# Cross-attention scores from stacked high and low parts, and a router that reads unsplit tokens, in a two-layer decoder on one core

## What is computed

```python
# E: cross-attention, 16 heads of 16 columns
q = (x @ Wq + bq);  k = (ctx @ Wk + bk);  v = (ctx @ Wv + bv)      # each split into 16 heads
attn = softmax(clip(q @ k.T * 16 ** -0.5, -1e4, 1e4))
x = layernorm(x + (attn @ v) @ Wo + bo)
# F: router and experts
gate = softmax(x @ gate_w)                       # 8 experts, top 2 of each token
...
```

## Time and profile before

| | us |
|---|---|
| median of 3 runs (1593.13 to 1594.19) | 1593.33 |
| the profiled execution, its own time | 1595.76 |
| its span (what the trace covers) | 1594.0 |
| stage E, first to last score reduction | 928.4 to 1194.7 |
| closing of the last two batches, up to the last scatter | to 1247 |
| stage F (experts) | from about 1260 |

### The profile page before, as it was taken

The page is one execution under the profiler, slowest core; times in us unless marked ns, Lnnn a source line. Parts: engine busy times, 40 slices in busy tenths (PEclk is TensorE's granted clock), DMA queues, the critical chain, the costliest instruction groups (busy, mean ns, idle before and its releaser), DMA issues.

```text
span 1594.0 us, 23807 instructions
## 1 busy us (share of the span) xinstructions
PE 1365.7 (86%) x9303; PEld 1151.7 (72%) x9303; DVE 1114.1 (70%) x1885; ACT 560.8 (35%) x1122; POOL 804.4 (50%) x751
## 2 busy tenths in 40 slices
PE   5787799989989989989989789988894299999990
PEld 5786678868877877877666567766664299999990
DVE  5888776686676667654545568877783488888886
ACT  2354311021121121113333334444342266666652
POOL 3333456556556655642101123544555478888852
PEclk8897799999999999999999979989886599999995
DMA  5100133223322322310000000000000466566624
GB/s 167 31 11 16 47 93 102 95 84 101 98 69 90 96 80 86 97 58 28 1 1 1 6 6 1 13 13 23 8 8 14 147 240 212 216 236 227 208 70 158
DMA packets 44974, 129.83 MB, mean 81 GB/s; under 512 B 8406, under 2 KB 23225, under 8 KB 38976
## 3 DMA queue, kind: packets, MB, share of 16 engines
q1 hardware_dynamic: 32688, 66.70, 13.3%
q0 software_dynamic: 12176, 61.63, 10.9%
HBM read 119.82 MB, written 10.31 MB: 82 GB/s over the span
## 4 chain that ended last, share of the span: by engine, by line
PE 60%; DVE 22%; issue 6%; ACT 5%; POOL 3%; DMA 2%; SPq 0%; ACTq 0%; DVEq 0%; POOLq 0%
PE bank L399 13%; PE bank L401 12%; PE bank L400 12%; PE bank L1204 8%; PE bank L407 4%; PE bank L1039 3%; PE bank L1098 2%; PE bank L1025 2%; DVE topE L1731 2%; DVE hid_hi L1604 2%; DVE shiftE L1738 2%; DVE hf L1623 1%; PE bank L1120 1%; ACT feat L1356 1%; PE bank L1052 1%
## 5 line engine op out<-in xcount | busy, mean ns | idle before, releaser
L1606 DVE TENSOR_TENSOR hid_lo<-hf,hid_hi 128x512 fp32r<-128x512 f32 x96 | 219.8, 2290 | 3.3
L526 POOL TENSOR_TENSOR wpiece_lo<-wraw,wpiece_hi 128x1024 fp32r<-128x1024 f32 x88 | 215.9, 2453 | 7.4
L399 PE MATMUL bank<-hid_hi,wpiece_lo 128*128 128x512 f32 x512 | 200.5, 392 | 10.8 <-DVE hid_lo L1606 10.8
L400 PE MATMUL bank<-hid_lo,wpiece_hi 128*128 128x512 f32 x512 | 199.3, 389 | 0.0
L401 PE MATMUL bank<-hid_hi,wpiece_hi 128*128 128x512 f32 x512 | 199.3, 389 | 0.0
L524 POOL TENSOR_SCALAR wpiece_hi<-wraw 128x1024 fp32r<-128x1024 f32 x88 | 94.1, 1070 | 195.0 <-PE bank L401 191.0
L1604 DVE CAST hid_hi<-hf 128x512 fp32r<-128x512 f32 x96 | 77.6, 808 | 123.2 <-ACT hf L1306 122.1
L1306 ACT ACTIVATE hf<-bank,ffn_scales 128x512 f32<-128x512 f32 x64 | 44.2, 690 | 291.2 <-PE bank L401 291.2
L433 POOL TENSOR_TENSOR lnM_rstd<-lnM_rstd,minus_half 128x2 f32<-128x2 f32 x24 | 16.9, 709 | 214.8 <-DVE lnM_rstd L427 195.6
L635 POOL TENSOR_SCALAR probE<-probE 128x1024 f32<-128x1024 f32 x64 | 66.6, 1042 | 112.7 <-ACT probE L1388 112.5
L399 PEld LDWEIGHTS bank<-hid_hi,wpiece_lo 128*128 128x128 f32 x512 | 96.1, 188 | 35.6 <-DVE hid_lo L1606 15.9
(11 more groups left out here) (327 smaller groups left out, 3887.8 us busy)
## 6 DMA issues: line engine op xcount, KB each, us to landing
wraw<-in_C_w SPq DMA_DIRECT2D x88, 512.0 KB, 3.6
yc<-y_rows SPq DMA_DIRECT2D x16, 256.0 KB, 5.4
ctx_raw<-in_ctxT SPq DMA_DIRECT2D x16, 192.0 KB, 2.9
xraw<-in_xT SPq DMA_DIRECT2D x8, 256.0 KB, 3.8
x_tok<-in_x SPq DMA_DIRECT2D x8, 256.0 KB, 4.2
x_rows<-x_tok SPq DMA_DIRECT2D x8, 256.0 KB, 2.1
out_x<-x_tok SPq DMA_DIRECT2D x8, 256.0 KB, 2.1
staging<-in_A_wqkv SPq DMA_DIRECT2D x1, 768.0 KB, 6.7
```

The lines of the kernel that those rows point to most:

```text
L399: pe.e.matmul(o, sl, mh, start=start and i == 0, stop=False)
L400: pe.e.matmul(o, sh, ml, start=False, stop=False)
L526: pool.e.tensor_tensor(pair[1], raw, f(pair[0]), ALU.subtract).then_inc(done, 1)
L1606: dve.e.tensor_tensor(lo[:, o, :], hf[o % 2][:, :], f(hi[:, o, :]), ALU.subtract).then_inc(s_hid, 1)
```

## The change

1. Scores. q and k are no longer evicted into the tiles that the scores read. ScalarE evicts each of them twice with the bias added: into `qk_hi` (rounded to fp32r) and into `qk_raw` (fp32). GpSimd subtracts to get `qk_lo`. SyncE writes both parts to internal memory in HBM (`split_qk`) and reads them back, rearranged: each head gets 64 partitions, four blocks of its 16 rows: high, high, low, low for q and high, low, high, low for k. One fp32r matmul over the 64 rows then sums all four products of parts. For each of q and k of a batch there are 2 writes (256 KB each) and 8 loads, each of 16 partitions by 8 KB (128 KB), in pieces of 1 KB; 160 DMAs in all. There is one `qk_raw`, `qk_hi`, `qk_lo`, so k's eviction waits for q's subtraction and q's writes.
2. k is no longer stored twice with zeros; heads come in plain order.
3. Router. In stage E ScalarE copies the transposed tokens straight from PSUM into `xtf`; the high and the low part are not made there, and GpSimd's sum is gone.
4. FIN's later steps move one round ahead. `prob_e` has four buffers instead of six. `mask_a` lies in another part of SBUF, and the small load of `of_parity` is gone.

Below, after the tiles, come the programs of GpSimd, SyncE, TensorE and ScalarE, in this order.

```diff
-        items.append((base + PAIRS + 8, 1, "FIN", (b,), (0, 2, 4, 6, 7, 9, 11, 11, 13)))
+        items.append((base + PAIRS + 8, 1, "FIN", (b,), (0, 2, 4, 6, 6, 8, 10, 10, 12)))
...
+        split_qk = ring(2, lambda i: nc.dram_tensor(f"split_qk{i}", (2, 2, D, S), F32, kind="Internal").ap())
...
-        q_e = ring(2, lambda i: sbe(f"qE{i}", [P, KC, S]))
-        k_e = ring(2, lambda i: sbe(f"kE{i}", [P, 2, KC, S]))
+        qk_raw, qk_hi, qk_lo = sbe("qk_raw", [P, KC, S]), sbe("qk_hi", [P, KC, S], F32R), sbe("qk_lo", [P, KC, S], F32R)
+        q_e = ring(2, lambda i: sbe(f"qE{i}", [P, PAIRS, S], F32R))
+        k_e = ring(2, lambda i: sbe(f"kE{i}", [P, PAIRS, S], F32R))
...
+                elif name == "PRE" and step < 3:
+                    b, = args
+                    n, u = 2 * b + step - 1, use["E", "qk"[step - 1], b]
+                    pool.wait_ge(u.drained, u.done)
+                    pool.wait_ge(w_qk, 32 * n)
+                    pool.e.tensor_tensor(qk_lo[:, :, :], qk_raw[:, :, :], f(qk_hi[:, :, :]), ALU.subtract).then_inc(s_qklo, 1)
...
-                    if step == 4:
-                        wait_xt(pool, "E", b)
...
-                        pool.e.tensor_tensor(xtf[:, :, :], f(xt_hi[:, :, cols]), f(xt_lo[:, :, cols]), ALU.add).then_inc(s_xtf, 1)
...
+            def stack_heads(b, which):
+
+                n, held = 2 * b + which, split_qk[b % 2][which]
+                if b >= 2:
+                    sp.wait_ge(l_qk[b % 2], 16 * 16 * (b // 2))
+                for part, (src, done) in enumerate(((qk_hi, s_qkhi), (qk_lo, s_qklo))):
+                    sp.wait_ge(done, n + 1)
+                    load(held[part].rearrange("(c p) s -> p c s", p=P), f(src[:, :, :]), w_qk)
+                sp.wait_ge(w_qk, 32 * (n + 1))
+                if b >= 2:
+                    old = use["E", "s", b - 2, PAIRS - 1]
+                    sp.wait_ge(old.filled, old.full)
+                for r in range(4):
+                    heads = held[(r % 2) if which else r // 2].rearrange("(j i d) s -> i d j s", i=2, d=DH)
+                    for i in range(2):
+                        load(f((k_e if which else q_e)[b % 2][(4 * i + r) * DH:(4 * i + r + 1) * DH, :, :]), heads[i], l_qk[b % 2])
...
-                    for key in "qk":
-                        pe.wait_ge(use["E", key, b].drained, use["E", key, b].done)
+                    pe.wait_ge(l_qk[b % 2], 16 * 16 * (b // 2 + 1))
                     pe.wait_ge(u.drained, u.turn)
                     for t in range(TT):
                         for i in range(2):
-                            c, par, g = e_head(p, i)
-                            rows = slice(32 * g, 32 * g + 32)
+                            rows = slice(i * 4 * DH, (i + 1) * 4 * DH)
                             o = u.ap[:, (i * TT + t) * S:(i * TT + t + 1) * S]
-                            made = pe.e.matmul(o, q_e[b % 2][rows, c, t * P:(t + 1) * P], k_e[b % 2][rows, par, c, :],
+                            made = pe.e.matmul(o, q_e[b % 2][rows, p, t * P:(t + 1) * P], k_e[b % 2][rows, p, :],
                                                start=True, stop=True)
...
+                    act.wait_ge(s_qklo, n)
+                    act.wait_ge(w_qk, 32 * n)
                     for c in range(KC):
-                        if step == 1:
...
+                        made = act.e.activation(qk_hi[:, c, :], u.ap[:, c * S:(c + 1) * S], ACT.Identity, bias=bias[:, c:c + 1])
+                    made.then_inc(s_qkhi, 1)
+                    for c in range(KC):
+                        made = act.e.activation(qk_raw[:, c, :], u.ap[:, c * S:(c + 1) * S], ACT.Identity, bias=bias[:, c:c + 1])
                     made.then_inc(u.drained, 1)
```

More of the change, by code:

```diff
@@ L248, in build @@
         resid = ring(3, lambda i: sb(f"resid{i}", [P, TT, D], F32, mid))
-        mask_a = sb("mask_a", [P, 3 * P], F32, mid)
         ctx_raw = ring(2, lambda i: sb(f"ctx_raw{i}", [CK, 2, S], F32, mid))
@@ L271, in build @@
         wqkv = hilo("wqkv", [P, KC, 3 * D], early)
+        mask_a = sb("mask_a", [P, 3 * P], F32, early)
         bqkv = sb("bqkv", [P, 6], F32, early)
@@ L330, in build @@
         ev, eo = hilo("ev", [CK, 2, D], part, "right"), hilo("eo", [P, KC, D], part, "right")
-        ebq, ebk, of_parity = sbp("ebq", [P, KC]), sbp("ebk", [P, 2 * KC]), sbp("of_parity", [P, 2])
+        ebq, ebk = sbp("ebq", [P, KC]), sbp("ebk", [P, KC])
         ebv, ebo = sbp("ebv", [P, D]), sbp("ebo", [P, D])
@@ L362, in build @@
         s_vone, s_prob = sem("e_ones"), sem("e_prob")
-        s_xtf, s_rm, s_re, s_rf, s_rb, s_rs, s_sh = (sem(f"r_{n}") for n in ("xtf", "m", "e", "f", "b", "s", "sh"))
+        s_qkhi, s_qklo, w_qk, l_qk = sem("e_qkhi"), sem("e_qklo"), sem("w_qk"), ring(2, lambda i: sem(f"l_qk{i}"))
+        s_rm, s_re, s_rf, s_rb, s_rs, s_sh = (sem(f"r_{n}") for n in ("m", "e", "f", "b", "s", "sh"))
         s_seen, s_slot = sem("r_seen"), sem("r_slot")
@@ L633, in pool_program @@
                     pool.wait_ge(u.drained, u.done)
-                    pr = prob_e[n % 6][:, :, :, :].rearrange("p i k s -> p (i k s)")
+                    pr = prob_e[n % 4][:, :, :, :].rearrange("p i k s -> p (i k s)")
                     pool.e.tensor_scalar(pr, pr, 1.0, 0.0, ALU.min, ALU.max).then_inc(s_prob, 1)
@@ L639, in pool_program @@
                     b, = args
-                    finish("E", step, b, ebo, l_eb, 80)
-                    if step == 4:
-                        wait_xt(pool, "E", b)
-                        if b:
-                            old = use["E", "l", b - 1]
-                            pool.wait_ge(old.filled, old.full)
-                        cols = slice(b * S, (b + 1) * S)
-                        pool.e.tensor_tensor(xtf[:, :, :], f(xt_hi[:, :, cols]), f(xt_lo[:, :, cols]), ALU.add).then_inc(s_xtf, 1)
-                    elif step == 6 and b < B - 1:
+                    finish("E", step, b, ebo, l_eb, 64)
+                    if step == 6 and b < B - 1:
                         one_hot(pool, b)
@@ L789, in sync_program @@
             load(ebo[:, :], a["E_bo"], l_eb)
-            load(of_parity[:, :], a["of_parity"], l_eb)
             sp.wait_ge(s_ew, 1)
@@ L802, in sync_program @@
                     load(ctx_raw[b % 2][:, :, :], a["ctxT"][:, :, b * S:(b + 1) * S], l_ctx[b % 2])
+                elif name == "PRE" and step < 3:
+                    stack_heads(b, step - 1)
                 elif name == "FIN" and step == 4:
@@ L1134, in tensor_program @@
                         pe.wait_ge(l_rt, 16 * 5)
-                        pe.wait_ge(s_xtf, b + 1)
+                        ux = use["E", "x", b]
+                        pe.wait_ge(ux.drained, ux.done)
                         pe.wait_ge(u.drained, u.turn)
@@ L1326, in finish @@
                     ln_apply(act, "M", B + n, b, resid[(B + n) % 3])
+                elif step == 3 and stage == "D":
+                    ln_hi(act, "M", B + n, b, use["D", "x", b])
                 elif step == 3:
-                    ln_hi(act, "M", B + n, b, use[stage, "x", b])
+                    u = use["E", "x", b]
+                    act.wait_ge(u.filled, u.full)
+                    if b:
+                        old = use["E", "l", b - 1]
+                        act.wait_ge(old.filled, old.full)
+                    act.e.activation(xtf[:, :, :], u.ap[:, :].rearrange("p (c t) -> p c t", c=KC), ACT.Identity).then_inc(u.drained, 1)
             for name, step, args in DS:
@@ L1693, in finish @@
                     ln_scale(dve, "M", k)
-                elif step == 3:
-                    ln_lo(dve, "M", k, b, use[stage, "x", b])
+                elif step == 3 and stage == "D":
+                    ln_lo(dve, "M", k, b, use["D", "x", b])
             for name, step, args in DS:
@@ L1723, in vector_program @@
                 if name == "PRE" and step == 3:
-                    dve.wait_ge(l_eb, 80)
+                    dve.wait_ge(l_eb, 64)
                     values("E", *args, ebv)
@@ L1951 @@
         proj[r:r + DH, h // 2, h % 2, :] = g[L1 + "attn_proj"][h]
-    of_parity = (np.arange(P)[:, None] // DH % 2 == np.arange(2)).astype(np.float32)
     laid = {
@@ L1957 @@
         "mask_d": np.concatenate([tri.T, np.ones((P, P), np.float32), tri.T], 1),
-        "of_parity": of_parity,
         "iota8": np.broadcast_to(np.arange(NE, dtype=np.float32), (P, NE)),
@@ L1980 @@
         "E_bq": cols(g[L1 + "xattn_bq"]),
-        "E_bk": np.where(of_parity[:, :, None] > 0, cols(g[L1 + "xattn_bk"])[:, None, :], 0).reshape(P, 2 * KC),
+        "E_bk": cols(g[L1 + "xattn_bk"]),
         "E_wv": rows(g[L1 + "xattn_Wv"], CK),
```

33 lines of the change are left out of this document (9 added, 24 removed).

## The result

| | before | after |
|---|---|---|
| median of the runs | 1593.76 us | 1704.76 us (1688.96 to 1712.03) |
| the profiled execution, its own time | 1595.76 | 1688.96 |
| its span | 1594.0 | 1687.2 |
| first and last score reduction | 928.4, 1194.7 | 942.3, 1297.8 |
| end of the last scatter | 1247.2 | 1337.6 |

The ratio of the changed kernel to the one before is 1.0685 (95% interval 1.0589 to 1.078): slower by 111 us at the median, by 93 in the profiled executions. One of the four executions of the kernel before took 1969.6 us and is left out of the ratio; the other three lay between 1593.13 and 1594.19. Measured again beside the experiments, at another time, it was 1.0589 (1.0519 to 1.0658).

A forecast was written before the change was run, and what follows sets the result against it. Neither engine was full: VectorE alternated between work and waits for scores. Start +26, batches 0 to 2 +40, 3 to 6 +24.6, batch 7 -1.5, router and closing -10: +79 on 1595.8, so 1674.9, median 1672; range 1585 to 1706 us.

The forecast's parts named there:

- batches 3 to 6: Stage E, later batches: period 43.5 us each, set by the way through memory, +24.6 us over 149.4.
- batches 0 to 2: Stage E, first batches: period 42.5 us each with the way through memory, +40 us over 87.5.
- L: Time of one set of eight loads of q or k: 12 us taken, between bounds 6.9 and 21.6.
- a wait put down to GpSimd's scatters instead of DMA: Sign of a wrong forecast: the wait for k in stage E comes from GpSimd's scatters, not DMA; no size given.
- time 0: Stage E: the scores of the round in which q is made; pair 0 is due five rounds later.
- The three rounds before time 0: Stage E, between a batch's pair 0 and the next time 0: about 9 us in batches 0 to 2, 10 later.
- Part 1: Scores on TensorE: cheaper by 0.56 us per pair; gain 2.4 us per batch in batches 3 to 6, 1.5 in batch 7.
- Part 3: Router and closing: router waits for GpSimd's sum shorten in the last two batches; -10 us, bounds 0 and -11.
- k episode: Later batches: ScalarE waits 4.8 us for a layer norm, evicts k in 1.9, v's products stand behind 3.1; disappears in the trip's wait.
- No cost: Stage E: extra evictions (0.8 us a batch), GpSimd's subtractions (1.3 a batch) and four `prob_e` cost nothing.
- Quick loads: Rival for q and k loads: L near 7, issue-bound, total about 1592 us (1584 to 1603); chance 0.20.
- The clock: Rival in stage E: TensorE stays at 1.2 GHz with less matmul work, +115 us, about 1708; chance 0.08.

The follow-up runs named there:

- run 2: Changed kernel with FIN's last step, which issues the four scatters, four rounds later (12 to 16); median 1669.95 us, ratio 1.0449.
- run 3: Changed kernel with Wq and Wk columns reordered: 2 KB write pieces, four loads per set of 32 partitions spaced four apart; median 1643.12 us, ratio 1.0302.
- run 9: Kernel before with only FIN's steps from the router on moved one round earlier; ratio 0.9916.
- run 5: Changed kernel without subtraction, writes and loads: q and k evicted straight into the tiles the scores read, with wrong values; median 1561.68 us, ratio 0.9773.
- run 6: Kernel before with only the router part (`xtf` copied from PSUM) and FIN's steps moved ahead; median 1574.37 us, ratio 0.9864.
- run 8: On top of run 7, q, k and v of a batch made one round earlier, batch 0 as before; median 1595.34 us, ratio 0.9984.
- run 7: Changed kernel with run 3's interleaved layout and the scatters two rounds later (FIN's last step 12 to 14); median 1613.85 us, ratio 1.0135.
- run 11: On top of run 8, two buffers each for the high, low and raw parts; median 1623.91 us, ratio 1.001.
- run 1: Changed kernel with each of a set's eight loads over all 128 partitions, scores reading wrong places; median 1636.89 us, ratio 1.0251.
- run 12: Kernel before, unchanged, measured and traced again; ratio 1.0004.

## Why the prediction was right, and where it was not

The forecast was 1672 with a range of 1585 to 1706; the median is 1704.76, just inside, with two of the four runs above it. The sign, the mechanism (TensorE and VectorE idle ahead of each pair 0 on k's loads) and the order of its size were right. The sum came near for a reason that is half luck: the load time was taken too long, and two costs in batches 3 to 6 too short. No batch had the forecast period of 42 to 44 us: batches 0 to 2 took 34.8 to 39.8, batches 3 to 6 50.1 to 56.1. And L lay at or below the lower end of the stretch from 10 to 14 that had most of the chance. One sign of being wrong was a wait put down to GpSimd's scatters instead of DMA: the profile puts it down to the loads, as forecast, but run 2 shows the scatters behind it.

| term | forecast | measured |
|---|---|---|
| L, one set of eight loads | 12 | 9.2 to 10.2 |
| start, from q's eviction to the first scores | +26 | +21.5 |
| batches 0 to 2 | +40 | +24.4 |
| batches 3 to 6 | +24.6 | +63.9 |
| batch 7 | -1.5 | +0.9 |
| router and closing | -10 | -12.7 |
| whole, profiled executions | +79 | +93.2 |

The measured rows add up to 98.0; about 5 less come from outside the steps: q's eviction began 6.9 us earlier in this trace than in the one before, stage F took 2.7 longer, the first reduction stood 0.7 nearer to the first scores.

- **L.** The middle of the bounds 6.9 and 21.6 was too high by 2. With L = 10 the prediction's own working gives +22 for the start and +28 for batches 0 to 2, and both are met within 4. The wide loads show the cause that no row before showed: 5.8 us for the same megabyte over all partitions. The Trainium skill's figure in "SBUF — State Buffer", Door 1: The DMA port swizzle, is 104 GB/s for partitions 0 to 15; the windows here show 132 GB/s, somewhat above it. The estimate of 10.1 us from it was the better guide only without the fixed 2, which the prediction had added and which brings it back to the middle of 12. What the same page says under "Can I just issue two DMAs to hit both halves?" agrees in the main: the eight loads of a set cover eight different blocks of partitions, and together they moved 132 GB/s; no run shows one such load by itself. The section allows all ports only to a transfer that spans all 128 partitions; loads of 32 partitions spaced four apart do span them, and moved 267 GB/s (932 to 936 of run 3).
- **Batches 3 to 6.** This is the step that failed. With L = 10 it gives +8.6; the trace shows +63.9. In batch 4 k's low part is issued 15.0 us after time 0 (1069.2, three rounds behind 1054.16), forecast 15.5: the waits up to there were costed rightly, the scatters' 4.9 us on GpSimd among them. But the write was then taken to land at 19.5 by L = 10 (21.5 in the forecast, behind q's loads), and landed at 30.1. That is 10.6 of the 16.6 us by which this batch exceeds its 39.5. The scatters were costed as time of GpSimd alone and not as DMAs. Late scatters give 22 us back, and 27 where the loads are quick.
- **The three rounds before time 0** were taken as 10 us in the later batches. They took 14.5 to 15.7, and 11.7 to 12.1 already in the kernel before. The line of FIN by itself makes them 14.6 (run 9), as it puts work of older batches there, and in turn makes the five rounds behind them shorter (20.8 to 23.8 instead of 24.8 to 27.0). So the moved steps, a gain by themselves, lengthen the stretch that precedes the trip and shorten the one that waits for it anyway. Against the 10 us taken it is about 5 for each batch: in batch 4, 40.2 from time 0 to the scores and 15.0 in front, where L = 10 gives 29.5 and 10.
- **Part 1**, cheaper scores: 11 us forecast; from the router part alone (0.9864) to no trip (0.9773) it is 0.9%, 15 us. The size was right within its noise (the two intervals leave some 8 to 22 us), and the place was not: batches 0 to 2 gained 6.5 (78.9 against 85.4), where I had given nothing, batches 3 to 6 only 1, in single traces. Of the 6.5, 6.1 lie in batch 0 (22.7 against 28.8), and there the granted clock differs: 0.92 from 932 to 945 in run 5, but 0.64 in run 6 (936 to 949) and 0.52 in the kernel before (932 to 945), with TensorE busy all of the 13 us each time. Why it fell less with the cheaper scores wasn't tried.
- **Part 3**: 10 us forecast in the closing, 12.7 in the changed kernel, 10.5 alone. That the moved steps also remove the k episode, for which the prediction gave nothing, was missed; it shows only where no trip covers it.
- **No cost**: run 5 has the four evictions each and four `prob_e`, and VectorE's waits are down to 14.4 us; nothing of a cost is seen. GpSimd's subtractions are not in that run.
- **Rivals.** Quick loads gave about 1592 in the forecast; with wide or spaced loads the kernel took 1637 and 1643, since this rival had no place for the delayed writes either. With these removed as well it was 1614, and one round more was needed for 1595. What spoke for it, yc's 4 MB in 8.46 us, was the time of issue: each landed up to 6.9 us after its issue, and they moved 321 GB/s (1562 to 1572). The clock was no cause of its own: it is 0.50 in the waits (933 to 941, 1092 to 1099) and 0.79 from 1000 to 1200, and with no trip it is 0.91 there, as before.

The 130 us between the changed kernel (1.0589) and no trip (0.9773) thus divide, by differences of ratios: 46 for the loads' layout, 27 for the scatters beside the transfers, 24 for the trip one round earlier, which is cover and fewer collisions with the scatters together, and 34 that remain in the best version of the trip. Some 14 of these are the first one, which nothing covers: 18.9 us from q's eviction to the scores in run 8, where the kernel before needs 4.6.

## What to carry to other kernels

A rearrangement through memory is priced by the partitions of each single transfer, not by the bytes of the set; order the data so that every transfer is spread over all of them, and count the rounds that cover the whole chain of write, wait and load. Before a new transfer enters the path, look for indirect DMAs in the same rounds: they cost others more than their own issue. After every move of either, look again what now falls together. When a change has several parts, run each alone; here one line of the schedule and one small edit were worth 22 us, and the main part hid it.

## What the runs showed of the hardware that was not expected

- Four indirect scatters of 128 codes each, issued by GpSimd, hold up plain transfers that are beside them. k's low part, issued 2.3 us behind the last of them, took 13.4 to 15.2 us in batches 4 to 6 instead of the 6.1 to 8.2 of batches 0 to 3, once 20.0 (run 3). Of q's loads in batch 4 the longest landed 10.9 us after its issue, and 6.6 with the scatters moved away (run 2). A set of k's loads took 13.5 and 11.1 instead of 6.4 (run 7). Loads that were 1.3 and 2.5 us ahead were not touched in run 7, but in run 11 sets 1.2 and 1.7 us ahead took 8.5 and 9.5, so how far ahead is enough isn't settled. The scatters are late too: in batch 4 they landed 12.0 to 17.3 us after their issue, in the kernel before after a median of 5.5 (13.2 at most). While k's write was outstanding the DMA engines were nearly empty (share 0.02, 1 GB/s, from 1092 to 1099). Beside loads it looked otherwise: in run 7 they were busy 0.65 and moved only 53 GB/s (1100 to 1107), against 0.73 and 208 GB/s from 1057 to 1062. What it is inside the DMA engines stays open; it wasn't tried. The Trainium skill's page "DMA: Bandwidth & Descriptors", in its section on queues, rings and completion order, says that each engine turns between its queues packet by packet. By that rule alone, 2 KB of codes would cost a neighbour little; these rows show 5 to 9 us.
- Eight loads of 16 partitions each fill the DMA engines (share 1.15) at 132 GB/s. With the wide loads they moved 246 GB/s at a share of 0.88 (934 to 937 of run 1). So the share says that engines are occupied, not that they move much.
- Measurements on different chips differ by as much as the smaller edits here: the kernel before took 1595 and 1596 us on two and 1614 and 1622 on two others. Whether it is the chip or the moment isn't shown. Of the 25.5 us by which the span of run 12 (1619.5) is above the first trace's, 13 lie behind the last scatter, where no edit of this study is.
